# Graph attention with a routed FFN on one core: fewer rows gathered ahead, a fourteenth gather in 70 of 119 steps

## The reference, cut to what matters

```
x: 12500 x 256; src, dst: 212500 edges sorted by dst, one self loop a node among them; H = 4 heads, C = 64
xn    = layernorm(x)
h     = xn @ W                                    # 12500 x 256
alpha = leaky_relu(a_src[src] + a_dst[dst])       # a_src, a_dst: h with two vectors a head
alpha = softmax over the edges of one dst
x     = x + relu(layernorm(segment_sum(alpha * h[src]) + bias))
xn    = layernorm(x)
router: softmax(mean(xn) @ Wr + br) -> two of 8 experts with weights
x     = x + layernorm(xn + sum of two experts gelu(xn @ W1 + b1) @ W2 + b2)
```

## Time and profile before

| | |
|---|---|
| median of 3 runs | 3560.18 us (3556.11 to 3560.54) |
| profiled execution | 3558.36 us, span 3556.7 us |
| busy share of the span | PE 72%, DVE 64%, ACT 51%, POOL 47% |
| costliest group on POOL | L723, 1547 gathers, 1489.3 us busy |
| costliest group on PE | L816, 3332 matmuls, 1011.5 us busy |
| granted clock of PE | 0.865 of full speed on average |
| DMA | 429.58 MB, mean 121 GB/s |

### The profile page before, as it was taken

How to read it: one execution, slowest core, us unless ns; L and a number is a source line. 1 busy time by engine, 2 the same in 40 slices (tenths; PEclk the granted TensorE clock), 3 DMA queues, 4 the chain that set the end, 5 groups by cost and what they waited for, 6 DMA issues and landing times. The chain is left out here.

```text
span 3556.7 us, 69785 instructions
## 1 busy us (share of the span) xinstructions
PE 2553.7 (72%) x13470; PEld 1841.2 (52%) x13470; DVE 2285.4 (64%) x9629; ACT 1803.3 (51%) x6009; POOL 1675.5 (47%) x1950
## 2 busy tenths in 40 slices
PE   3193666667766766676676666676666599999998
PEld 2172455455545545455454554554454366666666
DVE  2062677777667777767777776777777646666555
ACT  1061566666566666666666666666666422222211
POOL 7603666666666666666666666666666000000000
PEclk7596788888788898988888888889888799999999
DMA  7674444445444444544444444444444111111110
GB/s 232 205 214 142 132 139 135 133 133 140 132 137 137 138 133 135 143 135 132 136 137 135 140 139 135 140 136 136 138 140 130 54 51 36 36 36 41 36 41 32
DMA packets 256976, 429.58 MB, mean 121 GB/s; under 512 B 68737, under 2 KB 185729, under 8 KB 255617
## 3 DMA queue, kind: packets, MB, share of 16 engines
q0 software_dynamic: 81888, 244.40, 25.2%
q1 hardware_dynamic: 173386, 181.46, 16.4%
q10 hardware_dynamic: 1495, 1.95, 0.2%
HBM read 368.60 MB, written 59.03 MB: 120 GB/s over the span
## 5 line engine op out<-in xcount | busy, mean ns | idle before, releaser
L723 POOL DMA_INDIRECT rows<-table,idx x1547 | 1489.3, 963 | 434.6 <-issue 397.0
L816 PE MATMUL bank<-msg,oh 128*128 128x260 f32 x3332 | 1011.5, 456 | 150.8 <-issue 75.3
L816 PEld LDWEIGHTS bank<-msg,oh 128*128 128x128 f32 x3332 | 749.9, 230 | 338.9 <-issue 143.0
L1047 ACT ACTIVATE msg<-rows,we 128x65 f32<-128x65 f32 x1904 | 478.5, 333 | 0.4
L1337 DVE TENSOR_TENSOR msg<-rows,bank 128x520 f32<-128x520 f32 x595 | 381.6, 678 | 2.2 <-ACT msg L1047 0.9
L933 PE MATMUL bank<-rows,msg 128*128 128x256 f32 x1536 | 340.6, 378 | 0.0
L920 PE MATMUL bank<-rows 128*128 128x512 f32 x768 | 336.2, 595 | 4.4 <-DMA rows<-in_L_ffn_W 4.4
L1182 ACT ACTIVATE msg<-bank,b_sb 128x512 f32<-128x512 f32 (+1 forms) x200 | 134.5, 678 | 365.7 <-PE bank L920 347.9
L933 PEld LDWEIGHTS bank<-rows,msg 128*128 128x128 f32 x1536 | 288.4, 189 | 51.4 <-issue 10.6
L864 PE MATMUL bank<-ident_b,ohT 128*128 128x128 bf16 x1680 | 163.1, 271 | 173.3 <-issue 58.4
L1144 ACT ACTIVATE ln<-mv,eps 128x1 f32<-128x1 f32 x119 | 35.0, 294 | 452.2 <-DVE mv L1513 429.8
(11 more groups left out here) (222 smaller groups left out, 4177.4 us busy)
## 6 DMA issues: line engine op xcount, KB each, us to landing
dst_b<-dst SPq DMA_DIRECT2D x122, 448.0 KB
rows<-table,idx POOLq DMA_INDIRECT x1547
tab_w<-table SPq DMA_DIRECT2D x121, 134.5 KB
xe<-x_src SPq DMA_DIRECT2D x123, 128.0 KB
x_w<-in_x_rows SPq DMA_DIRECT2D x121, 128.0 KB
x_mid<-x_o SPq DMA_DIRECT2D x119, 128.0 KB
x_src<-rows POOLq DMA_DIRECT2D x9, 1664.0 KB
table<-msg SPq DMA_DIRECT2D x50, 269.0 KB
```

Of the source, the lines that this page charges most:

```text
L723: pool.indirect_dma_start(rows[:, slot, t, :], None, table, bass.IndirectOffsetOnAxis(ap=idx[slot][:, t:t + 1], axis=0), bounds_check=None ...
L816: mm = pe.matmul(psA, oh[:, of, t, :], msg[:, of, t, :], start=(t == 0), stop=(t == TILES - 1))
L1047: ins = act.activation(head_cols(msg[:, s, t, :])[:, h, :], head_cols(rows[:, at.slot(), t, 0:HC1])[:, h, :], ACT.Copy, scale=we[:, t, h:h ...
```

## The change

Raw rows of x are gathered for 51 chunks in place of 119, each gather but the first two behind a wait for the transposes of a pair (`T*`, two pairs back), and stored in 4 parts, each issued behind the second gather of the next part (the last behind the last gather). In the edge stage 49 steps take their fourteenth tile from them as before; in the other 70 POOL gathers it from `table` as well, and `hi` is 2 in place of 5, so that no engine does the work for raw rows. `walk` becomes a loop over turns with raw rows, on POOL one turn written out between (`late=2`), and a loop to turn 29 without a test; the old nested loops stand behind a test that is false here. The pair's DMAs give a partition two neighbouring rows. On DVE the marks of parts left out are skipped together, and the normalising of the first group is taken apart: statistics into the step `over_last`, the rest among the router's chain; PE's transposes of that group and DVE's copy of them come later too.

```diff
-X_FIRST = 2 * GATHERS
-WALK = 6
+WALK = 5
+def sure_rounds(chunks):
+    return ((chunks | RING - 1) - 3) // RING
...
+    X_ROUNDS = (PAIRS - 5) // RING
+    X_CHUNKS = X_ROUNDS * RING + 7
...
-        def walk(eng, total, step, long=False):
+        def walk(eng, total, step, long=False, late=0):
             for j in range(-4, 2):
                 step(At(0, RING, j), -j, 5)
-            with eng.Fori(0, (STEPS - 3) // RING, WALK) as far:
-                with eng.If(far * RING + 3 < total):
-                    with nc.Fori(far, far + WALK, engines=[eng.engine], hint_back_edge=long) as k:
-                        with eng.If(k * RING + 3 < total):
-                            for j in range(2, 2 + RING):
-                                step(At(k, RING, j), -2, 5)
-                    hold(eng, s_nested)
+            def four(k, late=RING):
+                for j in range(RING):
+                    step(At(k, RING, j + 2), -2, 5 if j < late else 2)
+            with nc.Fori(0, X_ROUNDS, engines=[eng.engine], hint_back_edge=long) as k:
+                four(k)
+            hold(eng, s_nested)
+            if late:
+                four(X_ROUNDS, late)
+            with nc.Fori(X_ROUNDS + (late > 0), SURE, engines=[eng.engine], hint_back_edge=long) as k:
+                four(k, 0)
+            hold(eng, s_nested)
+            with eng.If(total > SURE * RING + 3):
+                with eng.Fori(SURE, (STEPS - 3) // RING, WALK) as far:
...
+        def rows_landed(at, lead, hi):
+            if hi > 2:
+                return at.landed(GATHERS, lead)
+            return at.landed(TILES, lead) - 16 * len(range(at.slot(lead), X_ROUNDS * RING + 5, RING))
...
                 sp.dma_start(x_in[:, at.slot(lead), :, :],
-                             x[bass.ds(at.number(lead) * PAIR, PAIR), :].rearrange("(b p) d -> p b d", p=P))\
+                             x[bass.ds(at.number(lead) * PAIR, PAIR), :].rearrange("(p b) d -> p b d", b=2))\
...
-                sp.dma_start(table[bass.ds(at.number() * PAIR, PAIR), :].rearrange("(b p) c -> p b c", p=P),
+                sp.dma_start(table[bass.ds(at.number() * PAIR, PAIR), :].rearrange("(p b) c -> p b c", b=2),
...
-                    sp.wait_ge(s_rows[at.slot(1)], at.landed(GATHERS, 1))
+                    sp.wait_ge(s_rows[at.slot(1)], rows_landed(at, 1, hi))
...
-            def gather_x(i):
+            def gather_x(c):
+                i, r = divmod(c, GATHERS)
+                slot = i % (RING - 1)
+                if r == 0 and i >= RING - 1:
                     pool.wait_ge(s_xsrc[slot], 16 * (i // (RING - 1)))
                     hold(pool, s_granted)
+                if c > 1:
+                    p1_pe.wait(pool, "T*", each_pair(c - 2, c - 1)[0])
+                    hold(pool, s_granted)
...
+                if r == 1 and i > 0:
+                    store_x(i - 1)
...
-            gather_x(len(x_parts) - 1)
-            store_x(len(x_parts) - 2)
+            for c in range(X_CHUNKS - 6, X_CHUNKS):
+                gather_x(c)
+            store_x(len(x_parts) - 1)
...
             for j in range(PAIR_RING):
                 pool.wait_ge(s_tab[j], 16 * (len(range(j, PAIRS, PAIR_RING)) + 1))
             pool.wait_ge(s_dst16, 16)
-            store_x(len(x_parts) - 1)
...
-                for t in range(GATHERS):
+                n_tiles = GATHERS if hi > 2 else TILES
+                for t in range(n_tiles):
...
-            walk(pool, total, gather)
+            walk(pool, total, gather, late=2)
...
-                    act.wait_ge(s_rows[at.slot(2)], at.landed(GATHERS, 2))
+                    act.wait_ge(s_rows[at.slot(2)], rows_landed(at, 2, hi))
...
                 def mark(on, name, make):
                     if on:
+                        settle()
                         dve2.mark(name, make())
                     else:
-                        dve2.skip(dve, [name], at)
+                        left_out.append(name)
...
+                if beside:
+                    beside()
...
-            pe2.wait(dve, "agg", last)
-            hold(dve, s_dve_held)
-            normalise(At(0, 2, 0), At(0, 3, 0), 0)
-            step(over_last, -2, -1)
+            ahead2, ahead3 = At(0, 2, 0), At(0, 3, 0)
+            step(over_last, -2, -1, beside=lambda: stats_of(ahead2, ahead3, 0))
...
-            move_transposed(At(0, 2, 0), 0)
-            dve3.rest(dve, DVE3_A)
+            root_of(ahead2, -1, DVE3_A[2:])
+            pe2.wait(dve, "agg", over_last)
+            normalise_row(ahead2, ahead3, 0, 0)
```

More of the change, by code:

```diff
@@ L146, in build @@
     XO_ROWS = (GROUPS + 1) * GROUP
+    X_ROUNDS = (PAIRS - 5) // RING
+    X_CHUNKS = X_ROUNDS * RING + 7
+    assert 0 < X_ROUNDS < SURE and X_CHUNKS <= chunks and X_CHUNKS <= PAIRS + 2
     with ExitStack() as ctx:
@@ L319, in build @@
         s_win = [sem(f"s_win{i}") for i in range(RING)]
-        s_xidx = [sem(f"s_xidx{i}") for i in range(2)]
+        s_xidx = sem("s_xidx")
         s_xrow = [sem(f"s_xrow{i}") for i in range(RING - 1)]
@@ L418, in hold @@
             eng.sem_inc(counted, 1)
[L422 removed]
+        def walk(eng, total, step, long=False, late=0):
             for j in range(-4, 2):
                 step(At(0, RING, j), -j, 5)
[L425 to L431 removed]
+            def four(k, late=RING):
[11 more added lines that the diff above has]
+                with eng.Fori(SURE, (STEPS - 3) // RING, WALK) as far:
+                    with eng.If(far * RING + 3 < total):
+                        with nc.Fori(far, far + WALK, engines=[eng.engine], hint_back_edge=long) as k:
+                            with eng.If(k * RING + 3 < total):
+                                four(k, 0)
+                        hold(eng, s_nested)
         def among(lo, hi):
@@ L673, in store_x @@
                 hold(pool, s_granted)
[L674 to L680, removed]
+                pool.dma_start(x_src.rearrange("(q i) d -> q (i d)", i=X_CHUNKS)[:, part.start * D:part.stop * D],
+                               flat_rows[:, bass.ds((slot + 1) * slot_size, (part.stop - part.start) * D)])\
+                    .then_inc(s_xsrc[slot], 16)
+            pool.wait_ge(s_xidx, 16)
+            for c in range(X_CHUNKS // 6):
+                gather_x(c)
             pool.wait_ge(s_wide, 16)
             pool.tensor_scalar(narrow, wide, float(TOP16), None, ALU.min).then_inc(s_narrow, 1)
[L683 to L686, removed]
+            for c in range(X_CHUNKS // 6, X_CHUNKS - 6):
+                gather_x(c)
             total = steps_to_run(pool)
@@ L732, in _ @@
             hold(pool, s_granted)
-            for t in range(GATHERS):
+            for t in range(TILES):
                 pool.dma_start(spare[0:1, t:t + 1], src_t[0:1, t:t + 1]).then_inc(s_rows[RING - 1], 16)
@@ L973, in _ @@
             mm.then_inc(s_once, 1)
+            transpose_rows(At(0, 2, 0), 0)
+            pe3.rest(pe, ["xT"])
             pe.wait_ge(s_setup, N_TOP)
@@ L1309, in _, with step @@
             dve2.credit(dve, rounds=4)
-            def step(at, lo, hi):
+            def step(at, lo, hi, beside=None):
                 s, q = at.slot(0, 2), at.slot(-1, 2)
@@ L1549, in move_transposed, with moments_of @@
                 dve3.mark("xT", ins)
-            def rstd_of(at, lead, names, rows_of, n_q):
-                def own(name):
-                    dve3.wait(dve, name, at, lead)
+            def moments_of(at, lead, names, rows_of, n_q):
                 for q in range(n_q):
@@ L1558, in rstd_of @@
                 dve3.mark(names[0], ins)
-                own(names[0])
+                dve3.wait(dve, names[0], at, lead)
                 hold(dve, s_dve_held)
@@ L1669, in _ @@
             link(dve.tensor_copy(wtop[:, :], bank[5][:, 0:2]))
+            move_transposed(ahead2, 0)
+            dve3.rest(dve, DVE3_A)
             dve.wait_ge(s_fw2, 64)
```

81 lines of the change are left out of this document (47 added, 34 removed).

## The result

The changed kernel takes **3480.5 us** (median of 4 runs, 3476.6 to 3481.8) against 3558.1 us for the kernel before beside it (4 runs, 3556.1 to 3560.5): ratio 0.978, 95% interval 0.9763 to 0.9797. The profiled execution took 3480.22 us, its span is 3478.4 us, 78.3 us under the span before. Forecast were 3507 us and 53 us less, so the direction and the range held; but all three savings were larger than forecast, and so was the price of the fourteenth gather. One of the 31 executions of the kernel before in the third group of experiments took 6726 us and is left out there.

The account below looks back on a forecast made before the run. GpSimd's gathers and its marker waits for TensorE's signals were taken to set the edge step. Table stage -103, fourteenth gather +87.5, loop ends -21 and -3, tail -13.5 sum to -53: 3507 us against the median, range 3450 to 3555.

Parts of the forecast that it names:

- The sum for a step, 20.3 us: Edge stage: 13 gathers at 1.25 us, two markers at 0.34, and waits of 1.86 and 1.5 us make a step.
- Table stage, -103: Start to first edge-stage marker: 203 us in place of 305.9, with raw-row gathers cut from 119 to 51.
- the pair at 3.5 us: Table stage: a pair of row blocks takes 3.5 us, next to the 3.6 for moving 0.80 MB at 223 GB/s.
- rival (a): Table stage: the pair runs at PE's own pace, 2.4 to 2.9 us; -40 more, 3465 us; 10%.
- the sum's own case: Whole kernel: the forecast's terms hold as summed, 3507 us against the median, spread 3470 to 3545; 66%.
- Rival (b): Table stage stays slow: signals withheld, PE at the low clock, a pair 4.7 us or more; 3565 us; 10%.
- Fourteenth gather, +87.5: Edge stage: 70 steps get one more gather of 1.25 us each; +87.5 us.
- (c): Edge stage: a fourteenth gather costs nothing, as markers wait for a fixed PE and DVE chain; 3439 us; 8%.
- (d): Edge stage: a train of eight costs more than its gather, another 0.7 us a step; 3555 us; 6%.
- Loop ends, -21 and -3: Edge stage, every fourth step: longer second train covers half of DVE's delay, -21 us; inner loop's test removed, -3 us.
- Tail, -13.5: After the edge stage: guard -5, first group's normalising moved -7, marks skipped together -3, its return in the router's chain +1.5 us.
- Neighbouring rows, 5 us: Table stage: longer runs in loads of x and stores of the table save 0.1 us a pair.

Follow-up runs that it names:

- third group of experiments: Same-chip runs: kernel before 3044.3 us; with 64 never-run instructions ahead of VectorE's loops 3016.9; changed kernel 3036.1, with 48 such 3038.2, with trains of seven and seven 3033.0.
- the first two groups: Eight runs, each the changed kernel with a part undone or altered; kernel before 3554.8 us in one group, 3540.3 in the other; changed kernels 3387.8 to 3502.4 us.
- the first two runs: Changed kernel with the comparison k * RING + 3 < total put back inside the edge stage's loops: on all engines 3482.6 us, on VectorE alone 3486.4 us.

## Why the prediction was right or wrong, point by point

- **The mechanism** (GpSimd's trains of gathers set the step; TensorE's signals are seen when the train is over) held in the runs of the result and of the first two groups: a gather less is 1.35 us less, and the waits stay. The sum for a step, 20.3 us, is not quite what it says: it counts the 0.3 us behind the last gather of each train twice, in the 1.25 and in the wait. Without that it is 19.7, where plain steps took 20.2; nothing in the forecast hangs on it. That it always is so, as I wrote it ("whatever PE's lead"), is wrong: in the third group the same program has no such waits. Nothing in the profile before could have told.
- **Table stage, -103, was -113.9.** The failing step is the pair at 3.5 us "by the bytes at 223 GB/s", where I took the rate of one stretch for the limit of the DMA engines. They did 278 here, and 312 in the third group; the kernel before itself has stretches of 25 us at 243 and 244. The pair took 3.19 us in the mean, and without the three stalls behind the stores some 2.9, so rival (a) is as near as the sum's own case. From the last pair to the first marker it took 19 us, not 14. Rival (b) named the right place, a load of x behind a store with the low clock after it, but it happens in three pairs (and without the store in the one at 24 us), not in all.
- **Fourteenth gather, +87.5, was +95** (20.23 to 21.59 us a step, 70 times; 94.8 us when taken away). Rivals (c) and (d) are out.
- **Loop ends, -21 and -3, were about -47**: (20.63 - 20.23) x 118. The failing step is the sentence "if the loop's end itself became quick for DVE it would be -24 more over all the steps, and no row speaks for it". It became quick, and the steps of 13 gathers gained as well. The comparison to which I gave 0.3 us isn't the cause, as the first two runs show, nor the nesting; the packets of queue q14 and the shift of the kernel before show that it was a late fetch of instructions, which goes with the place in the program. That the changed kernel's loops fell on better places was luck; no part of the change aimed at it. With the longer steps' gathers at +95 and the loop ends at -47 the edge stage would be +48; +52.3 were measured, 3 of them one step of 24.7 us near the passage from the first loop to the second.
- **Tail, -13.5, was -16.6**, or -17.9 without the last train's eighth gather. DVE's exit from the loops went from 9.97 to 2.81 us, where I had given it 5; without the guard the tail is 3.4 us longer. The rest is as forecast within some 2 us.
- **Neighbouring rows, 5 us**: 4 to 10.
- **The spread of the sum's case** is added up too narrow: 3507 with -25 to +35 and -7 to +21 is 3475 to 3563, not 3470 to 3545, if both go the same way. The measured time lies inside either.

By stages the errors have one sign, -11, -11 and -3, and make up the difference of 25 us. The middle one is itself a difference: the loop ends brought 23 us more than forecast, the gathers and the passage took 11 back.

## What to carry to other kernels

Where an engine waits at a fixed distance behind another engine's burst of DMA issues, look for waits to set between the issues: with one gather a pair, pairs were 2.9 us apart outside the stalls against 2.4 without any, while under trains single pairs came 24 to 34 us apart. A loop whose end costs 2 us more than its instructions may be cured by moving it: look whether a packet of the instruction queue starts at the branch, and try some instructions ahead of the loop, never run, before rebuilding it. And measure a gain in more than one place: a change that trades work of GpSimd between stages won 2.2% in one and 0.25% in another.

## What the runs showed that I had not expected

The kernel before took 3540 to 3558 us in three places and 3044 in a fourth, and the changed one 3480 and 3036, with the same 0.95 us for a gather and a granted clock of 0.856 and 0.848. Of the 445 us between the two traces of the changed kernel 439 lie in the edge stage (2478.8 and 2039.4), 3.7 us a step, and the waits before the two markers, 464 us in one trace, are but the first one, 18 us, in the other. The best kernel differs with it: the changed one where signals come late (3480 against 3558), the kernel before with its loop moved where they come in time (3017 against 3036). The moved kernel was not run where they come late; by the 47 us of its loop ends it would be near 3511 there, an estimate. What decides between the two conditions stays open.
